# Base written before the routed rows, shared rows added in five pieces, one comparison in 16 bits, extra rounds ahead of the last aggregate

## What is computed

```python
def gnn(x, edge_index, eps, W1, b1, g1, be1, W2, b2, g2, be2):
    src, dst = edge_index[0], edge_index[1]            # 10625 edges, sorted by dst
    agg = jax.ops.segment_sum(x[src], dst, num_segments=N)
    h = (1.0 + eps) * x + agg
    h = relu(batch_norm(h @ W1 + b1, g1, be1))         # 512 -> 1024
    h = relu(batch_norm(h @ W2 + b2, g2, be2))         # 1024 -> 512
    return x + h

def ffn(x, ...):                                       # 64 experts, 6 per token, 2 shared
    shared = sum over 2 of silu(x @ sWg) * (x @ sWu) @ sWd
    gate = softmax(x @ Wr), top 6 of 64, divided by their sum
    routed = sum over 64 experts of (silu(x @ Wg[e]) * (x @ Wu[e]) @ Wd[e]) * gate[:, e]
    return shared + routed + x

x = x + gnn(layernorm(x), ...)
x = x + ffn(layernorm(x), ...)
```

## Time and profile before

| | us |
|---|---|
| median of 3 runs | 781.27 (780.87 to 785.67) |
| the profiled execution, its own time | 782.4 |
| its span in the trace | 780.7 |
| PE busy | 722.4 (93%) |
| DVE busy | 260.5 (33%) |
| ACT busy | 195.1 (25%) |
| POOL busy | 174.7 (22%) |
| HBM over the span | 301 GB/s |

### The profile page before, as it was taken

One profiled execution on the slowest core, in us unless ns is written; L12 is line 12 of the kernel. 1 busy time (PEld: TensorE's weight loads), 2 busy tenths in 40 slices (PEclk: granted clock), 3 DMA queues, 4 the chain that ended last, 5 costly groups with the idle time before them and its releaser, 6 DMA issues. The chain is left out here.

```text
span 780.7 us, 17521 instructions
## 1 busy us (share of the span) xinstructions
PE 722.4 (93%) x7096; PEld 478.5 (61%) x7096; DVE 260.5 (33%) x788; ACT 195.1 (25%) x497; POOL 174.7 (22%) x157
## 2 busy tenths in 40 slices
PE   2699999879999999999999999999999999489993
PEld 2597776556666666555566666655566666356662
DVE  7983524975221442222221212121233222012100
ACT  1222321402332222211222222121222333033331
POOL 4000000011222232232332222222333332123211
PEclk9999999999999999999999999999999999789996
DMA  9970021426999999999999999999999999999921
GB/s 265 407 280 3 0 108 62 166 75 222 354 341 337 347 387 382 392 392 380 385 387 390 378 401 377 384 394 389 383 384 372 373 374 368 342 369 364 337 36 23
DMA packets 57265, 236.35 MB, mean 303 GB/s; under 512 B 6171, under 2 KB 6335, under 8 KB 40286
## 3 DMA queue, kind: packets, MB, share of 16 engines
q1 hardware_dynamic: 46004, 211.33, 70.8%
q0 software_dynamic: 10144, 20.56, 11.4%
q10 hardware_dynamic: 1034, 3.30, 1.1%
HBM read 222.32 MB, written 12.83 MB: 301 GB/s over the span
## 5 line engine op out<-in xcount | busy, mean ns | idle before, releaser
L424 POOL DMA_INDIRECT xg<-x_tab,idx_sb x64 | 71.8, 1121 | 387.9 <-DVE idx_sb L942 220.0
L1368 PE MATMUL ps<-ring,xT 128*64 128x256 f32 x1296 | 156.5, 383 | 0.6 <-ACT xT L608 0.6
L439 POOL DMA_INDIRECT out<-ysb,idx_sb x64 | 92.5, 1445 | 202.4 <-DMA out<-ysb,idx_sb 124.4
L1368 PEld LDWEIGHTS ps<-ring,xT 128*64 128x64 f32 x1296 | 88.1, 137 | 43.8 <-issue 3.4
L628 ACT ACTIVATE ysb<-ps 64x256 f32<-64x256 f32 x64 | 24.2, 377 | 332.3 <-PE ps L1368 152.5
L935 DVE TENSOR_REDUCE gates<-ps 128x1 f32<-128x3 f32 (+1 forms) x62 | 10.0, 162 | 267.7 <-PE ps L1275 267.0
L1368 PE MATMUL ps<-ring,hTj 128*64 128x256 f32 x624 | 75.5, 384 | 0.0
L1368 PE MATMUL ps<-w,xT 128*64 128x256 f32 x608 | 75.1, 390 | 0.0
L903 DVE TENSOR_TENSOR onehot<-iotaAB,slotv 125x640 bf16<-125x640 f32 (+1 forms) x64 | 67.3, 1051 | 2.6 <-PE ps L1283 1.8
L999 DVE SCALAR_TENSOR_TENSOR hs<-hs,gates,ps 128x256 f32<-128x256 f32 x64 | 30.7, 480 | 90.2 <-PE ps L1373 43.8
L1368 PEld LDWEIGHTS ps<-ring,hTj 128*64 128x64 f32 x624 | 42.1, 136 | 30.1 <-issue 11.9
(11 more groups left out here) (237 smaller groups left out, 818.2 us busy)
## 6 DMA issues: line engine op xcount, KB each, us to landing
ring<-in_L_ffn_Wg SPq DMA_DIRECT2D x41, 1024.0 KB, 20.7
ring<-in_L_ffn_Wu SPq DMA_DIRECT2D x40, 1024.0 KB, 21.2
ring<-in_L_ffn_Wd SPq DMA_DIRECT2D x39, 1024.0 KB, 22.5
w<-in_L_ffn_Wd SPq DMA_DIRECT2D x20, 1024.0 KB, 22.4
w<-in_L_ffn_Wg SPq DMA_DIRECT2D x19, 1024.0 KB, 21.6
w<-in_L_ffn_Wu SPq DMA_DIRECT2D x19, 1024.0 KB, 21.3
ring_x<-in_L_ffn_Wu SPq DMA_DIRECT2D x5, 1024.0 KB, 20.2
ring_x<-in_L_ffn_Wd SPq DMA_DIRECT2D x5, 1024.0 KB, 20.3
```

What stands on the lines that cost most here:

```text
L424: g.indirect_dma_start(out=xg[j % NX][0:ROWS[j], :], out_offset=None, in_=x_tab, in_offset=bass.IndirectOffsetOnAxis(ap=idx_sb[0:ROWS[j], ...
L439: g.indirect_dma_start(out=out, out_offset=bass.IndirectOffsetOnAxis(ap=idx_sb[0:ROWS[j], j:j + 1].bitcast(u32), axis=0), in_=ysb[h][0:ROW ...
L1368: last = t_.matmul(ps[h * BIG:(h + 1) * BIG, bank, 0:AW], big(k), w[:, k, h * AW:(h + 1) * AW], start=(k == 0), stop=(k == KD - 1))
```

## The change

Four edits:

1. `out` isn't filled with zeros any more. SP writes the base from `x_sb` to `out` with two plain DMAs, after it has issued the thirteenth weight tile. Scatter 0 waits for them.
2. The shared experts' rows no longer add to the base: the first shared expert's result is copied to `x_sb`, the second's is added. POOL adds `x_sb` to `out` tile by tile, behind scatters 41, 45, 49, 53 and 57, each with two DMAs of 224 and 26 KB that accumulate. The scatter behind each waits for both to land.
3. `one_m` is compared from two tiles of 16-bit integers. `iota_m` is laid out over all 625 elements, and the column values, which were read as float32 with a broadcast, are first spread over 625 16-bit elements by ScalarE (`spread`, 25 passes) into ten buffers `rep`. Six of the ten lie in weight buffer 7, so SP issues the eighth weight tile only once all one-hots are there.
4. The branch to the extra rounds stands ahead of the last aggregate. The last block's columns of `hT` are set to zero on VectorE, and the last aggregate is added to them there, where ScalarE copied it before.

```diff
-    BASE_AFTER = 50
-    PRE = 3 * 16
+    SHARED_AFTER = [41, 45, 49, 53, 57]
+    NREP = 10
...
             for i, (r, j) in enumerate(items):
+                if i == 7:
+                    sp.wait_ge(s_sm, NG)
...
+                if i == 13:
+                    for a, b in PARTS:
+                        sp.dma_start(out.rearrange("(t p) d -> p t d", p=P)[a:b, :, :], x_sb[a:b, :, :]).then_inc(s_base0, 16)
...
-            g.dma_start(out[0:full * 128, :].rearrange("(t p) d -> p t d", p=128),
-                        zrows[:].unsqueeze(1).broadcast_to([128, full, D])).then_inc(s_pre, 16)
-            g.dma_start(out[full * 128:rest, :], zrows[0:EVEN, :]).then_inc(s_pre, 16)
-            g.dma_start(out[rest:N, :], zrows[0:N - rest, :]).then_inc(s_pre, 16)
...
-                if j == BASE_AFTER + 1:
-                    pool.wait_ge(s_base, 32)
+                if j == 0:
+                    pool.wait_ge(s_base0, 32)
+                if j - 1 in SHARED_AFTER:
+                    pool.wait_ge(s_base, 32 * (SHARED_AFTER.index(j - 1) + 1))
...
-            def add_base():
-
-                pool.wait_ge(s_sy, NS * T)
-                pool.wait_ge(s_scat[0], (BASE_AFTER + 2) // 2 * 16)
-                pool.wait_ge(s_scat[1], (BASE_AFTER + 1) // 2 * 16)
+            def add_shared(t, j):
+
+                pool.wait_ge(s_sy, (NS - 1) * T + t + 1)
+                pool.wait_ge(s_scat[0], (j + 2) // 2 * 16)
+                pool.wait_ge(s_scat[1], (j + 1) // 2 * 16)
                 for a, b in PARTS:
-                    g.dma_start(out.rearrange("(t p) d -> p t d", p=P)[a:b, :, :], x_sb[a:b, :, :],
-                                accum_op=ALU.add).then_inc(s_base, 16)
+                    g.dma_start(out[t * P + a:t * P + b, :], x_sb[a:b, t, :], accum_op=ALU.add).then_inc(s_base, 16)
...
-                if j == BASE_AFTER + LAG:
-                    add_base()
+                if j - LAG in SHARED_AFTER:
+                    add_shared(SHARED_AFTER.index(j - LAG), j - LAG)
...
+            def spread(b):
+                for g in range(b * GB, (b + 1) * GB):
+                    if g >= NREP:
+                        act.wait_ge(s_sm, g - NREP + 1)
+                    sc.activation(rep[g % NREP][:], col_m[:, g * U:(g + 1) * U].unsqueeze(2).broadcast_to([P, U, P]),
+                                  ACT.Copy).then_inc(s_rep, 1)
...
+                if spread:
+                    last = v.tensor_tensor(one_m[slot][:], iota_m[:], rep[g % NREP][:], ALU.is_equal)
+                else:
+                    last = v.tensor_tensor(one_m[slot][:], iota_m[:], col_m[:, c].unsqueeze(2).broadcast_to([P, U, P]),
+                                           ALU.is_equal)
...
+            v.memset(hT[:, :, (T - 1) * P:NP], 0.0).then_inc(s_hadd, 1)
             with dve.If(more_rounds > 0):
...
+            dve.wait_ge(s_hadd, 1)
+            dve.wait_ge(s_agg, T)
+            block = hT[:, :, (T - 1) * P:N]
+            v.tensor_tensor(block, block, ps[:, 4 + (T - 1) % 2, 0:KD * P].rearrange("p (k n) -> p k n", k=KD),
+                            ALU.add).then_inc(s_hT, 1)
...
+                    if e == 0:
+                        v.tensor_copy(x_sb[:, t, :], ps[0:P, 5, :]).then_inc(s_sy, 1)
...
             block_aggregate(T - 2)
-            block_aggregate(T - 1)
             with pe.If(more_rounds > 0):
...
+                pe.wait_ge(s_hadd, more_rounds * T + 1)
+            block_aggregate(T - 1)
```

More of the change, by code:

```diff
@@ L162, in gnn_moe_kernel @@
         aT = [rAT.place(f"aT{i}", [P, T, P], f32) for i in range(2)]
+        iota_m = rAT.place("iota_m", [P, U, P], i16)
+        rep = [rAT.place(f"rep{i}", [P, U, P], i16) for i in range(4)]
         rAT.rewind()
@@ L207, in gnn_moe_kernel @@
         cntS = rWin.place("cntS", [128, E], f32)
-        ring = [rOh.place(f"ring{i}", [128, KD, 512], f32) for i in range(8)]
+        ring = [rOh.place(f"ring{i}", [128, KD, 512], f32) for i in range(7)]
+        at_ring7 = rOh.at
+        ring.append(rOh.place("ring7", [128, KD, 512], f32))
+        rOh.at = at_ring7
+        for i in range(6):
+            rep.append(rOh.place(f"rep{4 + i}", [P, U, P], i16))
+        rOh.at = at_ring7 + 8192
         w2 = [rOh.place(f"w2_{i}", [128, KD, 512], f32) for i in range(2)]
@@ L256, in gnn_moe_kernel @@
             "vectors_T", "group_onehots", "group_visited", "aT_copied", "aT_ready", "h0_ready", "norm_ready", "extra_round"))
-        s_agg, s_hT, s_hpad = (sem(n) for n in ("aggregated", "hT_ready", "hT_padded"))
+        s_agg, s_hT, s_xagg, s_hadd = (sem(n) for n in (
+            "aggregated", "hT_ready", "extra_aggregated", "hT_added"))
         s_var, s_root = sem("variance"), sem("root")
@@ L313, in gnn_moe_kernel @@
         AFTER = min(j for j in unit_at if j > SPREAD + 5)
-        assert max(unit_at) < BASE_AFTER - 2
+        down_at = [j for j, u in sorted(unit_at.items()) if u[0] == NS - 1 and u[1] >= NGU]
+        assert all(j < b - 1 for j, b in zip(down_at, SHARED_AFTER))
         block = ctx.enter_context(nc.Block())
@@ L700, in columns, with group_onehots @@
                 return v.tensor_tensor(col_m[:], ps[0:P, 6, 256:256 + NV], grp_of[:], ALU.subtract)
-            def group_onehots(g, slot):
+            def group_onehots(g, slot, spread):
                 c = slice(g * U, (g + 1) * U)
-                for one, iota, col in ((one_s, iota_s, col_s), (one_m, iota_m, col_m)):
-                    last = v.tensor_tensor(one[slot][:], iota[:].unsqueeze(1).broadcast_to([P, U, P]),
-                                           col[:, c].unsqueeze(2).broadcast_to([P, U, P]), ALU.is_equal)
+                v.tensor_tensor(one_s[slot][:], iota_s[:].unsqueeze(1).broadcast_to([P, U, P]),
+                                col_s[:, c].unsqueeze(2).broadcast_to([P, U, P]), ALU.is_equal)
+                if spread:
+                    last = v.tensor_tensor(one_m[slot][:], iota_m[:], rep[g % NREP][:], ALU.is_equal)
+                else:
+                    last = v.tensor_tensor(one_m[slot][:], iota_m[:], col_m[:, c].unsqueeze(2).broadcast_to([P, U, P]),
+                                           ALU.is_equal)
                 last.then_inc(s_sm, 1)
@@ L787, in _ @@
                         for i in range(GB):
-                            group_onehots(b * GB + i, i)
-                        dve.wait_ge(s_agg, o * T + (T + b + 1))
+                            group_onehots(b * GB + i, i, False)
+                        dve.wait_ge(s_xagg, o * T + (b + 1))
                         block = hT[:, :, b * P:(b + 1) * P]
-                        v.tensor_tensor(block, block, ps[:, 4, 0:KD * P].rearrange("p (k n) -> p k n", k=KD),
-                                        ALU.add).then_inc(s_hT, 1)
+                        v.tensor_tensor(block, block, ps[:, 5, 0:KD * P].rearrange("p (k n) -> p k n", k=KD),
+                                        ALU.add).then_inc(s_hadd, 1)
+            dve.wait_ge(s_hadd, 1)
[3 more added lines that the diff above has]
+                            ALU.add).then_inc(s_hT, 1)
             v.tensor_tensor(x_sb[:], x_sb[:], h0[:], ALU.add).then_inc(s_acc0, 1)
@@ L1017, in unit @@
                     if i == 0:
-                        dve.wait_ge(s_acc, 1)
-                    if i >= T:
+                        dve.wait_ge(s_base0, 32)
+                    if e == 0:
+                        v.tensor_copy(x_sb[:, t, :], ps[0:P, 5, :]).then_inc(s_sy, 1)
+                    else:
                         dve.wait_ge(s_sy, i - T + 1)
-                    v.tensor_tensor(x_sb[:, t, :], x_sb[:, t, :], ps[0:P, 5, :], ALU.add).then_inc(s_sy, 1)
+                        v.tensor_tensor(x_sb[:, t, :], x_sb[:, t, :], ps[0:P, 5, :], ALU.add).then_inc(s_sy, 1)
             slot_onehot(0)
@@ L1113, in visits, with aggregate @@
                     visit(g, g % NSM, 2 * (b % 2))
-            def aggregate(from_aT, bank):
+            def aggregate(from_aT, bank, done):
                 for d in range(KD):
@@ L1119, in aggregate @@
                                          from_aT[:, s, :], start=(s == 0), stop=(s == T - 1))
-                last.then_inc(s_agg, 1)
+                last.then_inc(done, 1)
             def block_aggregate(b):
@@ L1127, in block_aggregate @@
                     pe.wait_ge(s_hT, b - 1)
-                aggregate(aT[b % 2], 4 + b % 2)
+                aggregate(aT[b % 2], 4 + b % 2, s_agg)
             pe.wait_ge(s_code, 2)
@@ L1165, in _ @@
             pe.wait_ge(s_hT, T)
-            pe.wait_ge(s_hpad, 1)
             for f in range(KH):
```

52 lines of the change are left out of this document (27 added, 25 removed).

## The result

The changed kernel takes **792.17 us** (median of 4 runs, 790.18 to 793.22) against 782.43 us before (4 runs, 780.87 to 785.67): a ratio of 1.0116, 95% interval 1.0076 to 1.0157. It is slower by 1.2%. The profiled execution took 793.22 us, its span is 791.5 us (before 782.4 and 780.7). The forecast was 792.5.

A forecast was written before the change was run, and what follows sets the result against it. TensorE's products were taken to bound the kernel behind the graph stage, VectorE before 54 us, with a nearly full scatter chain beside TensorE. Span 780.7 - 3.0 - 17.6 + 32 = 792.1, forecast 792.5 us, range 776 to 806.

The forecast's parts named there:

- The base write costs nothing: Start of the kernel, SP's queue: writing 1.25 MB of base into quiet DMA slices was costed at nothing.
- The 16-bit comparison at 0.40: Graph stage, VectorE: a 16-bit comparison takes 0.40 us instead of 0.73, saving 0.33 us per group.
- ScalarE's spread: Graph stage: ScalarE's passes keep up at 0.85 to 0.90 us each; the first block copy delays VectorE 0.8 us.
- 3.0 us saved at the head: Graph stage: W1 product starts at 60.4 us instead of 63.38, and all of the saving reaches the end.
- A piece costs 9.9 us: Expert stage, chain of scatters: each 125-row piece adds 9.9 us, bounds 8.2 and 11; five make 49.5.
- Room, thinner stream, tail: 5 + 9.5 + 3: Expert stage: off the pieces' 49.5 us come chain room 5, faster scatters beside fewer weights 9.5, last piece 3.
- 32 us of stall: Expert stage, TensorE: the pieces stall it 32 us in place of the one add's 17.6, so 14.4 lost.
- What would show it: Signs: W1 near 60.4 us, piece to next scatter about 10 then less, waiting copies, Silu pitches of 17 to 20.
- Fast pieces: Rival, expert stage: pieces cost 4 us of chain each, total 772.7 us; decides at about 6 us; chance 0.17.
- Nothing thins: Rival, expert stage: landings stay as slow as now whatever the load, total 805 us; chance 0.13.
- The stream thins sooner: Rival, expert stage: pieces land in 8.2 us, scatters fall to 8 after the second, total 782.7; chance 0.25.
- The 16-bit form brings nothing: Rival, graph stage: the 16-bit form or its feed gains nothing, adding 4 us to each case; chance 0.1.

The follow-up runs named there:

- Experiment 11: The kernel before, with its one add (base and shared rows) moved behind scatter 58 and a third output buffer: 769.15 us, ratio 0.9830.
- experiment 2: The kernel before, with only its add of base and shared rows cut into the five pieces: 791.58 us, ratio 1.0113.
- experiment 1: The changed kernel with its five pieces put back into one add of all shared rows behind scatter 50: 782.17 us, ratio 0.9996.
- experiment 4: The changed kernel without any add of the shared experts' rows (output incomplete): 771.92 us, ratio 0.9860.
- experiment 6: The changed kernel with its five pieces behind scatters 58, 59, 60, 61 and 62: 789.83 us, ratio 1.0079.
- experiment 10: The changed kernel with one add behind scatter 58, three output buffers, GpSimd's fills held back, a later spread wait, the last aggregate before the branch: 764.36 us.
- experiment 9: The changed kernel with both comparisons in the old float32 form and no spread passes on ScalarE: 797.94 us, ratio 1.0188.

## Why the prediction came out

**The base write costs nothing.** It went out at 151.39 us into DMA slices of 5 and 3, TensorE's wait for the first gather fell from 1.05 to 0.52 us, and scatter 0 stands 6.3 us behind its copy as before. Right.

**The 16-bit comparison at 0.40.** Right, 0.40 of pitch for 0.72. The Trainium skill's rule on it ("VectorE: DVE Perf Modes", section "What auto-detection actually checks") agrees with this row.

**ScalarE's spread.** It was put at 0.85 to 0.90 per pass and took 0.62 (ten in 6.24 us); the row it came from the earlier trace rows is of a pass with another output, and why this one is shorter wasn't tried. The step that failed is another: the prediction let VectorE start when it did before. It waits 0.89 us for the first spread tile, with both comparisons behind that wait, and its columns come 1.25 us late.

**3.0 us saved at the head.** Wrong: 1.0 at W1 (62.38 for 60.4), 0 at expert 1. Term by term: the start 2.1 us late (1.25 and 0.89), which no term of the sum held; the first aggregate at 30.01 for 28.7; the branch 1.79 for 1.3. Other executions spread: the seven other traces with this head have the W1 product at 60.96 to 62.33, the three with the head of before at 63.28 to 63.38, on average 1.6 us apart. What was left did not arrive. Silu 0 still comes 1.5 us earlier than before (168.24 for 169.76), Silu 1 doesn't (183.88 for 183.74). Expert 1's first 16 products, before and after:

```profile
173.16 1.95 PE L1368 MATMUL ps<-ring,xT 128*64 128x256 f32 x16
...
171.64 3.61 PE L1401 MATMUL ps<-ring,xT 128*64 128x256 f32 x16
```

TensorE's windows of the change (from:to, length, busy us, granted clock, DMA share, GB/s):

```profile
165.00:170.00 5.00, 3.29 (x58) 1.00 0.17 10
170.00:175.00 5.00, 4.48 (x40) 0.66 0.57 211
```

In the profiled execution of before, the second is at 1.00; in all the other traces but one it is at 0.50 to 0.72, with the head of before too (0.66 and 0.72, experiments 11 and 2). Behind short waits (for a gather, for ScalarE, for the gates: 0.5, 0.6 and 1.7 us) TensorE ran expert 1's products at the lower clock, and 16 of them took 3.61 us in place of 1.95. Experiment 11 has the head of before and the lower clock all the same, and its Silu 1 stands at 184.2 against 183.74. So this isn't the change's doing; it takes back a gain of one head against another in one pair of traces. Over the eight traces with the new head and the three with the old, Silu 1 is 0.4 us earlier on average, and the medians of experiments 1 and 2 are 0.4 us for and 0.6 against head and base together. Why the clock falls there in some executions and not in others stays open.

**A piece costs 9.9 us.** Near for four of five. Scatter j of the change less scatter j of experiment 4 shows the chain fall behind:

| scatter | 41 | 45 | 46 | 49 | 50 | 53 | 54 | 57 | 58 | 59 | 63 |
|---|---|---|---|---|---|---|---|---|---|---|---|
| later by, us | 1.2 | 12.1 | 22.8 | 22.6 | 31.4 | 25.4 | 35.8 | 37.7 | 38.4 | 33.0 | 30.9 |

The pieces add 10.8, 10.8, 8.8, 10.4 and 0.7, 41.5 in all, and not 49.5. The fifth meets hardly any other traffic (DMA share 0.44 and 70 GB/s from 751.0 to 756.4 us, against 1.03 and 351 beside the fourth): scatter 57 to 58 takes 9.75 us, and 9.1 in experiment 4, where weights are still under way.

**Room, thinner stream, tail: 5 + 9.5 + 3.** Too much: of the pieces' 41.5 us 29.5 reached TensorE, so 12.0 were taken off, and not 17.5. DMA issues of the change, 640 to 690 us (count, KB each, median us to landing):

```profile
ring<-in_L_ffn_Wd SPq DMA_DIRECT2D x3, 1024.0 KB, 9.3
...
out<-ysb,idx_sb POOLq DMA_INDIRECT x5, 8.2
```

The weights land in 9.3 us instead of 23.6, as forecast for behind expert 50: their queue is short. The scatters beside them still take 8.2, where the prediction let a fifth of them go at 5.9. A shorter queue did not make scatters faster; only where the weights pause did one follow in 5.15 us (684.47 to 689.62; DMA's share from 688 to 692 us is 0.34). That is most of the 6.0 us that came back between scatters 50 and 53; the end returned 7.5 behind 58.

**32 us of stall.** 231.88 - 202.4 = 29.5. The term was 2.5 too high: the pieces were put 8.0 too dear, and 5.5 too much was taken off them again.

**The sum.** -3.0 came out as 0, +14.4 as +11.9, and behind Silu 63 the change is 1.2 us shorter: 780.7 + 0.1 + 11.9 - 1.2 = 791.5 against the 792.1 of the sum. The forecast is right in its main mechanism, the pieces as links of a full chain, which experiments 1, 2, 4 and 6 show, and wrong on the head. That it hit within 1 us is luck: the head's gain of 3.0 us, which didn't reach expert 41, stands against 2.5 us put too high for the stall and 1.2 that the end gave back.

**What would show it.** Piece to next scatter 10.4 and 10.3 at the first two (570.88 to 581.25, 617.22 to 627.52), and 10.0 at the third, hardly less; copies that wait for scatters; Silu pitches of 17.4, 18.5, 18.8 and 14.3 at experts 46, 50, 54 and 58. The first of them, 7.2 us above the 10.2 without a piece, comes five experts behind its scatter: what stands between chain and TensorE took the rest.

**The rivals.** Fast pieces: the price it needed, 6 us, exists only without weights (4.8, experiment 6). Nothing thins (805): the chain did gain back 13.5 us. The stream thins sooner (782.7): it needed scatters at 8 us behind the second piece, and there (46 to 49) they stand 8.6 to 10.3 apart. The 16-bit form brings nothing: it brings 5.8.

## What to carry to other kernels

A chain of dependent transfers is paid per link: cutting one accumulation of 625 rows into five nearly doubles its price (from 21 to 41 us beside the weights, from 13 to an estimated 24 without), so cut it only where each link fits into room that is measured there. Ask first where the chain has room (here behind the last weights) and how many buffers stand between chain and engine; place and a third buffer turned a loss of 1.2% into a gain of 2.2%; with a quieter head it is 2.5%, which the intervals don't separate from 2.2. And when an edit takes work off one engine's start, look at what now coincides with the instructions beside it.

## What the hardware showed that was not expected

- A VectorE TENSOR_SCALAR of 125 elements took 1.80 us where two GpSimd fills of 1.01 and 1.13 us ran beside it, and 0.22 with the fills held back (experiment 10). It ended at 6.72, the second fill at 6.64. All nine traces with this order show 1.80. The Trainium skill, "SBUF — State Buffer", section "Who interferes with whom", says that `tensor_scalar` can take a port pair shared with GpSimd, for which the loser waits in full: these rows agree, and the wait went on through both fills. A comparison of two inputs beside the same fills (sel, 6.69 to 6.98 in experiment 10, the first fill from 6.63) kept its 0.29 us.
- The same accumulation takes 20.3 us to the next scatter under a full stream of weights and 12.1 to 12.7 at its end; a piece of 125 rows, counted the same way, takes 10 and 5.2 (757.20 to 762.41 in experiment 6).
- With the untaken conditional between two aggregates TensorE stands idle for 1.33 to 1.79 us there (nine traces; in six of them the profile has ScalarE's copy end the wait). Ahead of W1 the gap was 1.85 us in experiment 10, and 1.33 in the kernel before, in the same place. In experiments 9 and 10 the granted clock of 60 to 64 us, behind the gap, was 0.73 and 0.71; in the change it stayed at 1.00.
- Without any accumulating direct transfer the program ended some 9 us later behind its last landing than with one, all of it in GpSimd's closing DRAIN (10.5 us for 1.0 to 1.8); not explained, and seen in one kernel only.
